# Neighbour maximum with one pick per source chunk and the other neighbours fetched from subset tables

## The chip, the cores and the metric

The kernel runs on one core of one Trainium2 chip. The metric is the device time of one launch in microseconds. A core has a matrix engine (PE, with a weight-load side, PEld), a vector engine (DVE), an activation engine (ACT), a general engine (POOL, which also issues indirect DMAs), a sync engine (SP, which issues the plain DMAs) and 16 DMA engines.

## The reference, cut to what matters

A graph of 4096 nodes with 128 features passes through two layers. `adj` is a symmetric 0/1 matrix, int32, with ones on its diagonal; a row has about 17 ones.

```python
h = relu(layernorm(x))
x = x + max over the neighbours j of node i of h[j]        # layer 0: out[i, d] = max_j adj[i, j] ? h[j, d] : -inf
h = relu(layernorm(x))
x = x + elu(softmax(leaky_relu(s_i + t_j), over adj[i] > 0) @ (h @ W))   # layer 1, s = h W a1, t = h W a2
```

## The kernel before, in words

**Stage one, the neighbour maximum.** The work is cut into 8 tiles of 512 target nodes, and each tile into 16 steps of 256 source nodes (two chunks of 128), so 128 steps, counted by `g` (PAIRS). A step goes through these hands:

- SP (L262 to L285) loads 512 targets x 512 sources of `adj` (1 MB) for every two steps, four loads ahead, and writes the turned edges (0.5 MB for two steps) to DRAM as `edge_units`, for stage two.
- PE `flip` (L574) transposes eight 128x128 blocks, and ACT `edges` (L386) turns them into 0/1 `edge_t`, sources on the partitions. PE `rank` (L589) multiplies with a triangular matrix, so that `order_ps` says how many edges stand above each edge in its chunk.
- ACT `select` (L393) makes from it `first` (the first edge of each target in each chunk, a one-hot selector) and `depth`. DVE `seconds` (L845) makes the selector `second`, and DVE `rests` (L852) and ACT `later` (L405), in turn, make `rest`: the edges that are neither first nor second.
- PE `pick(g, 0)` and `pick(g, 1)` (L598) multiply `first` and `second` with h in two fp16 halves (`h_hi`, `h_lo`), four 512-column matmuls each, and each pick is the feature row of one neighbour. DVE `take` (L858) raises the running maximum `acc` with each of the two (128x1024, float32); `fold` (L869) closes a tile.
- PE `digest` (L617) packs the rest edges of four chunks into one number for each position in a chunk: a word of four bits, 1024 words for each target. ACT `key` (L413) moves it to `keys` as the row number in a table. DVE `search` (L873) takes the 8 largest of the 1024 words of 128 targets with one MAX8.
- The table `subset_max` in DRAM holds the maximum of h over every subset of four rows. It is made in the first tile: DVE `chain` (L837), 11 maxima of 128x1024, and POOL, which writes it out (L335 to L347). POOL then fetches 6 rows for each target, as 6 indirect DMAs of 128 rows x 512 B for each block of 128 targets, paced by `raised`, the count of takes (L357 to L364). DVE `halve_two` and `halve` (L877, L891) reduce them to `left`, in a ring of NG = 4 blocks.

**Between the stages** the picks are transposed (`rows`, L631), merged with `left` (`merge`, L970), added to x and normalised again.

**Stage two, the attention**, is 256 steps `n` in the hand-written ORDER: DVE `weigh` (L1047) makes a 128x512 weight tile, and PE `mix` (L696) multiplies it with 129 columns of float32. DVE may be 6 tiles ahead (WEIGHTS). What is left of stage one is set between the steps by hand, in DVE's own order (L1083 to L1143): the searches of the last three blocks at n = 12, 33 and 44, joins at 19, 46, 56, 58, 62 and 68, `merge(6)` at 50. At the end a flag is summed up. If a row was not covered by its fetches, all engines enter a loop that does stage one again, one edge rank at a time.

Every engine works in program order. DVE's order is written by hand, so a wait in a `halve` holds back the `take` behind it; `pick` waits for the `take` that frees its PSUM buffer.

```python
pe.wait_ge(raised, 2 * (g - 1) + k + 1)                        # L609, in pick(g, k)
pool.wait_ge(raised, 2 * (STEPS + 2 + QUAD * n) + 4 + s)       # L359, the pace of the fetches
dve.wait_ge(gathered[b % NG][k], 16 * FETCHES // 2 * (b // NG + 1))   # L882, in halve_two
```

## Time and profile before

| | before |
|---|---|
| median of 3 runs | 742.18 us (742.01 to 743.37) |
| profiled execution, span | 753.0 us |
| PE busy | 681.6 us, 91% |
| DVE busy | 693.7 us, 92% |
| ACT busy | 473.1 us, 63% |
| POOL busy | 281.8 us, 37% |
| DMA moved | 163.07 MB |

The page gives one profiled execution: its span from the first to the last instruction is 753.0 us, and it states no other time of its own; the runs without a profile take 742.18 us. Busy time counts an engine's instructions, not its waits, and matmuls are shown longer than the spacing at which they follow each other, so spacings are read from the timeline. Stage one fills the first 27 of the 40 slices, stage two the others.

### The profile page before, as it was taken

The numbers are of one execution on the slowest core, as the hardware profiler recorded it, in microseconds if no ns is written. First come the engines' busy times: TensorE is split into PE (matmuls) and PEld (weight loads), VectorE is DVE, ScalarE is ACT, GpSimd is POOL, SyncE is SP. The second block draws the span as 40 slices with busy tenths as digits, with TensorE's granted clock in tenths as the row PEclk, the third lists the DMA queues.
The fourth block names the chain that finished last, engine by engine and source line by source line (L and its number), as shares of the span: only waits on it lengthen the run. The fifth ranks groups of instructions, "written<-read, shape, count | busy, mean of one in ns | idle before, by whom it ended". The sixth has DMA issues, their size and how long they took to land.

```text
span 753.0 us, 14749 instructions
## 1 busy us (share of the span) xinstructions
PE 681.6 (91%) x5560; PEld 490.6 (65%) x5560; DVE 693.7 (92%) x1023; ACT 473.1 (63%) x685; POOL 281.8 (37%) x259
## 2 busy tenths in 40 slices
PE   1788999999999999999999998699999999999994
PEld 1344655555555555555555554498998999999994
DVE  8999999999999999999999999988998999889893
ACT  3888999889898899998999897562433111001000
POOL 0612034434434535444444355441620294134040
PEclk9999999999999999999999999799999999999998
DMA  9999978997888888888888746342531544443400
GB/s 305 310 355 390 344 230 270 303 327 239 268 249 247 273 258 237 272 265 241 261 263 265 246 143 228 103 143 71 187 130 62 219 140 158 156 177 130 165 15 17
DMA packets 63000, 163.07 MB, mean 217 GB/s; under 512 B 6416, under 2 KB 11152, under 8 KB 58832
## 3 DMA queue, kind: packets, MB, share of 16 engines
q1 hardware_dynamic: 53776, 138.75, 54.2%
q0 software_dynamic: 9152, 23.34, 12.1%
q8 instruction: 47, 0.77, 0.4%
q14 instruction: 25, 0.20, 0.1%
HBM read 117.51 MB, written 44.56 MB: 215 GB/s over the span
## 4 chain that ended last, share of the span: by engine, by line
PE 53%; DVE 31%; issue 12%; ACT 2%; DMA 1%; DVEq 0%; another core or an unknown queue 0%; SPq 0%
PE pick_ps L714 23%; DVE acc L867 20%; PE pick_ps L613 17%; DVE rest L1054 5%; PE late_ps L627 4%; PE late_ps L585 4%; PE order_ps L594 2%; PE late_ps L693 1%; PE late_ps L623 1%; DMA best<-x 1%; DVE left L889 1%; ACT depth L403 1%; DVE found L915 1%; PE late_ps L714 1%; PE order_ps L680 1%
## 5 line engine op out<-in xcount | busy, mean ns | idle before, releaser
L867 DVE TENSOR_TENSOR acc<-pick_ps,acc 128x1024 f32<-128x1024 f32 x248 | 302.6, 1220 | 20.9 <-PE pick_ps L613 12.6
L363 POOL DMA_INDIRECT found<-subset_max,tops x192 | 204.4, 1065 | 271.8 <-DVE acc L867 187.5
L1054 DVE SCALAR_TENSOR_TENSOR rest<-depth,curves_sb,stage 128x512 f32<-128x512 f32 x256 | 199.5, 821 | 15.3 <-PE pick_ps L714 3.1
L714 PE MATMUL pick_ps<-keys,rest 128*128 128x129 f32 x1792 | 207.7, 276 | 3.3 <-DVE rest L1054 3.2
L714 PEld LDWEIGHTS pick_ps<-keys,rest 128*128 128x128 f32 x1792 | 204.6, 193 | 7.4 <-DVE rest L1054 5.8
L402 ACT ACTIVATE first<-order_ps 128x1024 f16<-128x1024 f32 x128 | 131.9, 1030 | 39.1 <-PE order_ps L594 33.0
L403 ACT ACTIVATE depth<-order_ps 128x1024 f16<-128x1024 f32 x128 | 131.5, 1027 | 0.0
L613 PE MATMUL pick_ps<-first,h_hi 128*128 128x512 f16 x256 | 97.3, 380 | 17.6 <-DVE acc L867 17.1
L613 PE MATMUL pick_ps<-second,h_hi 128*128 128x512 f16 x256 | 97.2, 380 | 15.2 <-DVE acc L867 14.7
L585 PEld LDWEIGHTS late_ps<-ident_h,stage 128*128 128x128 f16 x1024 | 68.4, 99 | 50.0 <-DMA stage<-adj 12.9
L613 PE MATMUL pick_ps<-first,h_lo 128*128 128x512 f16 x256 | 97.4, 380 | 0.0
L613 PE MATMUL pick_ps<-second,h_lo 128*128 128x512 f16 x256 | 97.3, 380 | 0.0
L585 PE MATMUL late_ps<-ident_h,stage 128*128 128x128 f16 x1024 | 80.2, 223 | 16.5 <-DMA stage<-adj 12.9
L594 PE MATMUL order_ps<-edge_t,order_w 128*128 128x512 f16 x256 | 77.6, 385 | 4.2 <-ACT depth L403 3.0
L391 ACT ACTIVATE edge_t<-late_ps 128x512 int32<-128x512 int32 x128 | 78.0, 610 | 4.2 <-PE late_ps L585 4.2
L627 PE MATMUL late_ps<-bit_w,rest 128*128 128x128 f16 x1024 | 78.4, 220 | 0.1
L516 ACT ACTIVATE keys<-pick_ps,acc 128x128 f32<-128x128 f32 x28 | 8.0, 367 | 97.7 <-DVE acc L1065 97.7
L613 PEld LDWEIGHTS pick_ps<-second,h_hi 128*128 128x128 f16 x256 | 24.8, 97 | 67.0 <-issue 45.5
L411 ACT ACTIVATE rest<-depth 128x1024 f16<-128x1024 f16 x64 | 68.3, 1067 | 0.0
L627 PEld LDWEIGHTS late_ps<-bit_w,rest 128*128 128x128 f16 x1024 | 64.4, 98 | 5.4 <-issue 0.8
L371 POOL TENSOR_SCALAR keys<-keys 128x512 f32<-128x512 f32 x7 | 12.9, 1845 | 111.2 <-ACT keys L516 111.1
L613 PEld LDWEIGHTS pick_ps<-first,h_hi 128*128 128x128 f16 x256 | 24.9, 97 | 39.4 <-issue 19.1
(146 smaller groups left out, 599.9 us busy)
## 6 DMA issues: line engine op xcount, KB each, us to landing
stage<-adj SPq DMA_DIRECT2D x64, 1024.0 KB
edge_units<-edge_t SPq DMA_DIRECT2D x64, 512.0 KB
stage<-edge_units SPq DMA_DIRECT2D x32, 1024.0 KB, 4.8
subset_max<-keys POOLq DMA_DIRECT2D x13, 512.0 KB, 9.0
found<-subset_max,tops POOLq DMA_INDIRECT x192
best<-x SPq DMA_DIRECT2D x4, 512.0 KB, 5.9
subset_max<-x POOLq DMA_DIRECT2D x4, 512.0 KB, 6.6
out<-keys POOLq DMA_DIRECT2D x7, 256.0 KB, 2.8
```

Source lines behind the costliest of these rows:

```text
L363: nc.gpsimd.indirect_dma_start(found[:, n % NG, s, :], None, subset_max, bass.IndirectOffsetOnAxis(tops[:, n, s:s + 1], 0)).then_inc(gathe ...
L391: nc.scalar.activation(edge_t[:, g % (KEPT * KEEP), :].bitcast(I32), flip_i[:, :], ACT.Copy, scale=ONE_BITS).then_inc(edge_ready, 1)
L402: nc.scalar.activation(first[:, g % 4, :], order_ps[:, :], ACT.Relu, scale=-1.0, bias=1.0 - MARK).then_inc(first_ready, 1)
L403: nc.scalar.activation(depth[:, g % 4, :], order_ps[:, :], ACT.Abs, bias=MARK - MID).then_inc(depth_ready, 1)
L411: nc.scalar.activation(rest[:, to, :], depth[:, g % 4, :], ACT.Sigmoid, scale=-SHARP, bias=SHARP * (MID - 1.5)).then_inc(rest_odd, 1)
L585: last = nc.tensor.transpose(flip_ps[:, c * TI + r * P:c * TI + (r + 1) * P], low[:, (s * PAIR + c) * P:(s * PAIR + c + 1) * P], ident_h[: ...
L594: last = nc.tensor.matmul(order_ps[:, c * TI:(c + 1) * TI], order_w[:, :], edge_t[:, g % (KEPT * KEEP), c * TI:(c + 1) * TI], start=True, ...
L613: last = nc.tensor.matmul(pick_ps[k][:, c * TI:(c + 1) * TI], half_h[:, p * PAIR + c, :], s[:, c * TI:(c + 1) * TI], start=part == 0, stop ...
L627: last = nc.tensor.matmul(key_ps[:, r * P:(r + 1) * P], rest[:, g % RESTS, c * TI + r * P:c * TI + (r + 1) * P], bit_w[:, b, :], start=n % ...
L714: last = nc.tensor.matmul(out_ps(q, b), weight[:, n % WEIGHTS, b * P:(b + 1) * P], wh[:, c, :], start=c == 0 and starts(q, b), stop=c == C ...
L867: V.tensor_tensor(acc[:, q % 2, :], pick_ps[k][:, :], acc[:, q % 2, :], ALU.max).then_inc(raised, 1)
L1054: V.scalar_tensor_tensor(out=weight[:, n % WEIGHTS, :], in0=limit[:, q % 4, :], scalar=slope[:, c:c + 1], in1=units[:, m % EDGES, k * TI:( ...
```

## The change

- `depth`, `second` and `rest` are gone. There is one pick per chunk (`pick(g)`), with two PSUM buffers in turn, and one `take` per step.
- The words are made of all edges minus the first ones: `digest` multiplies `edge_t` with `bit_w` and `first` with its negative `bit_n`, 16 small matmuls for each step in place of 8. The word numbers (`ones_h` with `word`, 512 columns) are added for every group of four chunks, not for every second one.
- `key` becomes a Relu with a sum beside it (`key_sums`), into a ring of eight 128x512 groups.
- The search goes by 512 sources: `maxes` takes the best 8 of 128 words for each block of 128 targets and each group (four MAX8 for two steps). `rank_words` then takes the best 8 of the 64 kept ones, makes row numbers of them, strikes them out (match_replace) and takes the next 8.
- 8 rows are fetched for each target in place of 6 (`SLOTS`), at most two fetches a step, and three for blocks 24 to 27, and the halving works on 8 slots.
- Rows with more than 8 words are listed apart ("spill"), in three parts (blocks 0 to 15, 16 to 23, 24 to 31): flags, counting matmuls, a permutation for each block (128x128, float32), a list of at most 128 rows for each part, 8 more fetches for the list, a scatter to DRAM, a load back and a maximum into `left`. The DRAM table `spill_max` is cleared by four more writes of 512 KB in the first tile.
- The flag for the loop at the end is raised if a row has 16 or more words, if a group held more than 8, or if a list is longer than 128.
- In stage two the order on DVE and PE moves: searches at n = 7, 11, 13, joins at 5, 33, 40, 46, 56, `merge(6)` at 58, spill steps at 14 to 18, 28, 50 and 58, and PE's `columns(6)` and `project(6)` from 60 and 63 to 66 and 69.

```diff
 SLOTS = 8
-FETCHES = 6
+RANKS = 16
...
+                for i in range(4):
+                    nc.gpsimd.dma_start(spill_dram[:, i * EIGHTH * 2:(i + 1) * EIGHTH * 2, :], spare(3)).then_inc(spill_clear, 16)
...
+                def spill_fetch(k):
+                    pool.wait_ge(spill_listed, k + 1)
+                    if k == 1:
+                        pool.wait_ge(spill_best, 1)
+                    for s in range(SLOTS):
+                        nc.gpsimd.indirect_dma_start(spill_found[k][:, s, :], None, subset_max,
+                                                     bass.IndirectOffsetOnAxis(spill_rows[:, k, s:s + 1], 0)).then_inc(spill_in, 16)
...
                 for n in range(C):
+                    q, r = n // ROWS, n % ROWS
+                    if n in (16, 24, 31):
+                        spill_fetch((16, 24, 31).index(n))
+                    if n in (18, 26):
+                        spill_store((18, 26).index(n))
+                    if n in (19, 27):
+                        spill_load((19, 27).index(n))
...
-                    pool.wait_ge(topped, n + 1)
+                    pool.wait_ge(ranked, n + 1)
                     if n >= NG:
                         pool.wait_ge(reduced, n - NG + 1)
-                    for s in range(FETCHES):
-                        if n < LAST * ROWS - 1:
-                            pool.wait_ge(raised, 2 * (STEPS + 2 + QUAD * n) + 4 + s)
+                    for s in range(SLOTS):
+                        if q < LAST:
+                            pool.wait_ge(raised, STEPS * (q + 1) + 4 + (r * SLOTS + s) // (2 if q < LAST - 1 else 3))
+                        elif n > LAST * ROWS or s >= 3:
+                            b, t = (n, s - 3) if s >= 3 else (n - 1, SLOTS + s - 3)
+                            pool.wait_ge(gathered[b % NG][t % 4], 32 * (b // NG) + 16 * (t // 4 + 1))
...
                 def select(g):
                     act.wait_ge(ordered, g + 1)
-                    nc.scalar.activation(first[:, g % 4, :], order_ps[:, :], ACT.Relu, scale=-1.0, bias=1.0 - MARK).then_inc(first_ready, 1)
-                    nc.scalar.activation(depth[:, g % 4, :], order_ps[:, :], ACT.Abs, bias=MARK - MID).then_inc(depth_ready, 1)
+                    if g >= FIRSTS:
+                        act.wait_ge(picked, g - FIRSTS + 1)
+                        act.wait_ge(digested, 2 * ((g - FIRSTS) // 2 + 1))
+                    nc.scalar.activation(first[:, g % FIRSTS, :], order_ps[:, :], ACT.Relu, scale=-1.0, bias=1.0 - MARK).then_inc(first_ready, 1)
...
                 def key(n):
                     act.wait_ge(digested, 2 * n + 2)
+                    if n >= KEYED:
+                        act.wait_ge(maxed, ROWS * (n - KEYED + 1))
+                    nc.scalar.activation(key_ring[:, n % KEYED, :], key_ps[:, :], ACT.Relu, bias=float(n % GROUPS - LEAST),
+                                         accum_out=key_sums[:, n:n + 1]).then_inc(keyed, 1)
...
+                def pick(g):
+                    pe.wait_ge(first_ready, g + 1)
+                    if g >= 2:
+                        pe.wait_ge(raised, g - 1)
...
                 def digest(n, half):
                     if half == 0:
-                        rest_done(pe, n)
+                        pe.wait_ge(first_ready, 2 * n + 2)
                         if n >= 1:
                             pe.wait_ge(keyed, n)
+                        nc.tensor.matmul(key_ps[:, :], ones_h[:, :], word[:, :].rearrange("p (r w) -> p r w", r=1).broadcast_to((P, ROWS, P)), start=True, stop=False)
                     for r in range(half * ROWS // 2, (half + 1) * ROWS // 2):
                         for b in range(QUAD):
+                            nc.tensor.matmul(key_ps[:, r * P:(r + 1) * P], edge_t[:, g % (KEPT * KEEP), at:at + P], bit_w[:, b, :], start=False, stop=False)
+                            last = nc.tensor.matmul(key_ps[:, r * P:(r + 1) * P], first[:, g % FIRSTS, at:at + P], bit_n[:, b, :],
+                                                    start=False, stop=r == ROWS - 1 and b == QUAD - 1)
...
+                    if g in (74, 106):
+                        pe.wait_ge(keyed, g // 2)
+                        spill_count((74, 106).index(g))
+                        pe.wait_ge(spill_seen, (74, 106).index(g) + 1)
+                    if g in (80, 110):
+                        pe.wait_ge(keyed, g // 2)
+                        spill_list((80, 110).index(g))
+                        pe.wait_ge(spill_listed, (80, 110).index(g) + 1)
...
+                def maxes(n, half):
+                    q, g = n // GROUPS, n % GROUPS
+                    dve.wait_ge(keyed, n + 1)
+                    for r in range(half * ROWS // 2, (half + 1) * ROWS // 2):
+                        V.max(best_words[:, q % 2, r, g * SLOTS:(g + 1) * SLOTS], key_ring[:, n % KEYED, r * P:(r + 1) * P]).then_inc(maxed, 1)
...
+                def rank_words(n):
+                    sort_step(V.max(tops[:, n, 0:SLOTS], of))
+                    sort_step(V.scalar_tensor_tensor(out=vacant[:, 1, :], in0=tops[:, n, 0:SLOTS], scalar=0.0, in1=vacant[:, 0, :], op0=ALU.is_equal, op1=ALU.mult))
+                    V.scalar_tensor_tensor(out=rows_at[:, n, :], in0=tops[:, n, 0:SLOTS], scalar=float(LEAST), in1=vacant[:, 1, :],
+                                           op0=ALU.add, op1=ALU.add).then_inc(ranked, 1)
+                    sort_step(V.match_replace(of, tops[:, n, 0:SLOTS], of, -1.0))
+                    sort_step(V.max(tops[:, n, SLOTS:RANKS], of))
...
                 for g in range(PAIRS):
+                    take(g)
+                    if g >= 3:
+                        maxes((g - 3) // 2, (g - 3) % 2)
+                    if q >= 1 and 3 <= p < 7:
+                        rank_words(ROWS * (q - 1) + p - 3)
+                    if q >= 1 and p >= 13 and q < LAST:
+                        halve(ROWS * (q - 1), 2, p - 13)
+                    if q >= 2 and 5 <= p < 8:
+                        halve(ROWS * (q - 2) + 2, 2, p - 5)
+                    if q == LAST and 11 <= p < 14:
+                        halve(ROWS * (q - 1), 2, p - 11)
+                    if g in (88, 121):
+                        spill_join((88, 121).index(g))
```

## Rows read from the trace of the kernel before

**Rows 1.** The page: span, busy time of each engine, and the chain that ended last.
```profile
span 753.0 us, 14749 instructions
PE 681.6 (91%) x5560; PEld 490.6 (65%) x5560; DVE 693.7 (92%) x1023; ACT 473.1 (63%) x685; POOL 281.8 (37%) x259
PE 53%; DVE 31%; issue 12%; ACT 2%; DMA 1%; DVEq 0%; another core or an unknown queue 0%; SPq 0%
```

**Rows 2.** Windows: us, PE, PEld, DVE, ACT, POOL busy (instructions), granted clock, DMA share, GB/s.
```profile
60.00:70.00 10.00, 8.61 (x73) 4.92 (x72) 9.90 (x11) 8.29 (x12) 1.60 (x3) 1.00 1.04 405
...
140.00:160.00 20.00, 18.38 (x144) 10.21 (x142) 18.82 (x20) 17.51 (x24) 8.15 (x9) 1.00 1.02 336
...
341.60:355.40 13.80, 12.80 (x107) 7.26 (x105) 12.40 (x13) 12.44 (x17) 6.25 (x6) 1.00 0.83 257
```

**Rows 3.** DVE around step 80: timeline from 306 us (start, length), and all folds.
```profile
306.48 1.22 DVE L867 TENSOR_TENSOR acc<-pick_ps,acc 128x1024 f32<-128x1024 f32 x1
307.61 0.68 DVE L850 TENSOR_SCALAR second<-depth 128x2048 f16<-128x2048 f16 x1
...
312.21 0.69 DVE L871 TENSOR_TENSOR best<-acc 128x512 f32<-128x512 f32 x1
...
L871 DVE TENSOR_TENSOR best<-acc x8: 682/686/687, 90.6 to 539.6; 128x512 f32<-128x512 f32 x8
```

**Rows 4.** PE in one step: timeline from 312.84 us, and eight weight loads.
```profile
312.84 0.38 PE L613 MATMUL pick_ps<-second,h_hi 128*128 128x512 f16 x1
...
313.70 0.61 PE L585 MATMUL late_ps<-ident_h,stage 128*128 128x128 f16 x8
314.15 0.61 PE L627 MATMUL late_ps<-bit_w,rest 128*128 128x128 f16 x8
314.60 0.38 PE L613 MATMUL pick_ps<-first,h_hi 128*128 128x512 f16 x1
...
461.90 0.65 PEld L627 LDWEIGHTS late_ps<-bit_w,rest 128*128 128x128 f16 x8
```

**Rows 5.** Groups of instructions by line: busy us, mean ns, idle before. DVE and ACT.
```profile
L402 ACT ACTIVATE first<-order_ps 128x1024 f16<-128x1024 f32 x128 | 131.9, 1030 | 39.1 <-PE order_ps L594 33.0 <-issue 3.2 <-remote 1.9
L391 ACT ACTIVATE edge_t<-late_ps 128x512 int32<-128x512 int32 x128 | 78.0, 610 | 4.2 <-PE late_ps L585 4.2
L875 DVE MAX8 tops<-keys 128x8 int32<-128x1024 f32 x32 | 39.0, 1218 | 0.0
L985 DVE BATCH_NORM_STATS2 acc<-x 128x6 f32<-128x128 f32 x32 | 6.9, 281 | 0.0
L1002 DVE TENSOR_TENSOR acc<-acc 128x4 f32<-128x4 f32 (+1 forms) x6 | 1.0, 164 | 0.2
```

**Rows 6.** DMA queues on the page, and the fetches on POOL (group by line, then timeline).
```profile
q1 hardware_dynamic: 53776, 138.75, 54.2%
...
L363 POOL DMA_INDIRECT found<-subset_max,tops x192 | 204.4, 1065 | 271.8 <-DVE acc L867 187.5 <-issue 44.3 <-DVE tops L875 20.7
...
316.63 0.95 POOL L363 DMA_INDIRECT found<-subset_max,tops  x1 [0.92 <-DVE acc L867]
317.89 0.95 POOL L363 DMA_INDIRECT found<-subset_max,tops  x1 [0.31 <-issue]
...
531.19 4.34 POOL L363 DMA_INDIRECT found<-subset_max,tops  x1 [0.96 <-DMA found<-subset_max,tops]
```

**Rows 7.** The chain that ended last, in order of time: the first and the last take.
```profile
27.36 1.23 DVE acc L864
...
477.10 1.23 DVE acc L867
```

**Rows 8.** Stage two: DVE's timeline at its start and before n = 72, and a stretch of PE's chain.
```profile
486.11 1.42 DVE L1054 SCALAR_TENSOR_TENSOR rest<-depth,curves_sb,stage 128x512 f32<-128x512 f32 x2
...
569.72 8.04 DVE L1054 SCALAR_TENSOR_TENSOR rest<-depth,curves_sb,stage 128x512 f32<-128x512 f32 x12
...
663.72 28.58 PE pick_ps L714 x256
```

More of the change, by code:

```diff
@@ L747, in _ @@
                 rows(3)
-                for half in range(2):
-                    digest(PAIRS // 2 - 1, half)
                 project(0)
@@ new lines, in spill_cuts @@
+                def spill_cuts(k, lo, hi):
+                    first_block, end = SPILLS[k]
+                    dve.wait_ge(spill_seen, k + 1)
+                    if k == 1 and lo == first_block:
+                        dve.wait_ge(spill_done, 1)
+                    for n in range(lo, hi):
+                        last = V.tensor_scalar(spill_perm[k][:, n - first_block, :], places[:, :], spill_at[:, n:n + 1], None, ALU.is_equal)
+                    if hi == end:
+                        last.then_inc(spill_cut, 1)
@@ new lines, in _, with halve @@
+                halves = [0]
+                def halve(n, blocks, i):
+                    at = slice(n % NG, n % NG + blocks)
+                    if i == 0:
+                        for b in range(n, n + blocks):
+                            for k in range(4):
+                                dve.wait_ge(gathered[b % NG][k], 32 * (b // NG + 1))
+                        V.tensor_tensor(found[:, at, 0:4, :], found[:, at, 0:4, :], found[:, at, 4:8, :], ALU.max).then_inc(halved, 1)
+                        halves[0] += 1
@@ L1041, in _ @@
                 scales(1)
+                maxes(QUADS - 2, 1)
+                for half in range(2):
+                    maxes(QUADS - 1, half)
                 def cap(q):
```

386 lines of the change are left out of this document (210 added, 176 removed).

## The prediction

> **What bounds the kernel now.** I read the page first: PE and DVE are each busy for over nine tenths, and the chain that ended last runs mostly over these two [rows 1]. A share over 753 us says nothing of a stage, so next the folds: DVE closes a tile at 90.6 us and another, four tiles later, at 312.21 [rows 3], so 16 steps take 55.4 us and a step 3.46. Stage one runs from the first take at 27.4 to the last at 477.1 us [rows 7], 60% of the span, and nearly all of the change is there.
>
> Then what each engine needs for a step. PE, from its timeline [rows 4]: four 512-column matmuls take 0.86 us (0.215 each) and sixteen 128-column ones 0.90 (0.056 each). Ten large and sixteen small make 3.05, and a quarter of a word matmul 0.05: 3.10 us. DVE: a take follows the last after 1.13 us (307.61 less 306.48) [rows 3]; two takes, half a `second`, a quarter each of a `rest` and a MAX8 and the halving make 3.3, and with a gap where two takes follow each other, 3.46: **DVE bounds the step**, PE is 10% behind, ACT has two activations of 1.03 us, one of 0.61, half a `key` (taken as 0.61, since it is as wide) and half a `later` of about 1.03: 3.5 by durations and less by spacing [rows 5]. DMA is busy at 0.83 in the steady windows [rows 2].
>
> **What the change makes of a step.**
> - PE: four pick and two rank matmuls, 6 x 0.215 = 1.29; 8 flips and 16 digests, 24 x 0.056 = 1.34; half a word matmul, 0.11. Together **2.74 us**. The second pick goes (0.86) and 8 small matmuls come (0.45).
> - DVE: one take 1.14. `maxes` adds two MAX8 of 128 columns. Not in the trace; from below it is bounded by the smallest operation (0.16), from above by MAX8 of 1024 (1.22) [rows 5]. Nearest is the 128-column statistics, 0.28 long; I take 0.21 as spacing, 0.42 a step. `rank_words` has five small operations that wait for each other, 64 columns or 8; match_replace is not in the trace, between 0.16 and 1.22, nearest the small end. I take 1.1 to 1.3 us for a block, 0.3 a step. Halving on 8 slots, two pairs of blocks a tile: 2 x 2.1 us = 0.26 a step, and the fold 0.04. Together **2.2 us**. The trace shows no DVE bound left, though it bunches at p = 5 and 6 to 3.8 us.
> - ACT: 1.03 + 0.61 + 0.31 and a sum beside the key, unseen, between nothing and a second pass of 0.62 for two steps: **2.0 to 2.3**.
> - DMA: the plain queue moved 138.75 MB in 54.2% of 753 us, so 340 GB/s while busy [rows 6]. A step's `adj` and edges are 0.786 MB, 2.31 us at full share. The window at 0.83 of 3.46 us holds 2.87, which leaves 0.56 for 1.5 fetches, 0.37 each. Two fetches make 2.31 + 0.75 = 3.06. The share has gone to 1.04 (405 GB/s) and 1.02 with fetches (336 GB/s) [rows 2], so **2.9 us**, with 2.26 as the low end (0.917 MB at 405 GB/s).
> - POOL: a fetch takes 1.065 us and waits 0.30, and back to back it is 1.26 (317.89 less 316.63) [rows 6]. Two a step: **2.5 to 2.7 us**.
>
> So PE 2.74, DMA 2.9 and POOL 2.6 take DVE's place, all within a tenth. I take 2.9 for a step; the ends are 2.74 and 3.1.
>
> **The sum, stage one.**
> 1. Start: ACT leaves out three `depth` before the first pick, but the scaling of x on DVE holds it nearly as long: -1.5 us (bounds -2.8 and +1 for the new constants).
> 2. First tile, 63.2 us to the fold. The tables (17 x 0.524 MB) and the new clearing (2.1 MB) go through the same queues as 17 steps of 0.786 MB; four loads (4.2 MB) may be used up. 20.2 MB at 385 GB/s (a little under the 405 of [rows 2]) are 52.5 us: -10.5. Bounds: 46.6 by PE, 63 unchanged.
> 3. 96 steps to the fold before the last tile: 6 x 55.4 = 332.4 against 278.4: -54.
> 4. Fetches behind the list. `spill_fetch` puts 8 fetches ahead of block 16, and POOL has no slack. From take 82 it needs 8 x 1.0 + 16 x 1.27 + about 3 us to land = 31.3; DVE reaches the halving of block 16 at step 93 after 29.6: +2 to +3. In the last tile the same 31.3 us stand against 8.15 steps (22.8 us), since halving is at p = 11: DVE waits **8.5 us** before the take behind it, and so does PE.
> 5. List on PE: counting 16 and 8 tiny matmuls (1.3), listing 24 float32 ones at 0.22 (5.3; by the float32 pace of stage two, 28.58 us for 256 halves [rows 8]), waits for DVE behind them 2.5: 9 us. DMA goes on loading meanwhile; I keep half, +4.
> 6. The last 15 steps: 54.1 us before (477.1 less the fold at 90.6 + 332.4); 42 + 9 (from 4) + 2 for the merges: -1.
>
> Stage one: -1.5 - 10.5 - 54 + 3 + 4 - 1 = **-60 us**.
>
> **Stage two.** DVE goes from 486.1 to 569.7 without rest [rows 8]: it bounds the first 72 steps, PE the others (256 halves in 28.58 us, 0.89 a step against 0.67 to 0.75 on DVE). Removed from DVE there: three MAX8 (3.7), six joins of 1.2, the old flag: 12 us. Added: three `rank_words` 3.6, five joins 9.5, eight 128x128 cuts 2, take and join of the list 2.4, `spill_merge(2)` 1.2, the flag's eight operations 1.8, marks 0.4: 21. Of the 9 to 10 more I count 8; later PE has no slack to give them back. Before n = 0 come six `maxes` and `spill_merge(1)`: +2.5. If POOL's last fetches come late, `spill_merge(2)` holds DVE another 0 to 6; I take 0. Together **+10.5 us** (4 to 18).
>
> **Sum:** -49.5. The profiled execution has a span of 753.0 us, 10.8 over the median of 742.18; I carry the difference over unscaled: 742.2 - 49.5 = 692.7, said as **693**. A measurement can tell about 0.2%, 1.5 us, from no change.
>
> **Rivals.**
> - **A, PE alone is the bound.** The DMA share is packet time, not a limit; packets overlap, and 405 GB/s has been seen. Then a step is 2.76, the 96 steps save 67.5, the first tile 14, and POOL keeps up: 742 - 1.5 - 14 - 67.5 + 9 + 4 - 3 + 6 = **675**; with stage two nearly unchanged, 668. Chance 0.27.
> - **B, DMA fetches get dearer when it is full.** A share of 1.04 then costs each fetch 0.5, a step is 3.15, each halving waits: 111 steps x 0.25 over the forecast: **720**. For it: one fetch took 4.34 us [rows 6]. Chance 0.1.
> - **C, slower.** POOL's fetches set the pace of DVE: every `halve` stands ahead of a `take`, and POOL is in order. From a spacing of 1.7 us for a fetch on (a step of 3.35, 49 us over 111 steps) the gain is gone; at 1.9 the time is 742 + 43 = **785**. Against it: 1.26 to 1.37 in the trace. Chance 0.04.
> - **D, weight loads bound the small matmuls.** Eight loads stand in the trace over 0.65 us [rows 4], 0.08 each, more than the 0.056 of the matmuls. In a run of 24 they could be what counts: 24 x 0.08 + 1.40 = 3.3 us a step, 111 x 0.4 over the forecast, **737**. Against it: sixteen in a row kept 0.056 [rows 4]. Chance 0.03. The Trainium skill (TensorE: Matmul & The Clock Gate, Back-to-back issue gap) says that a stream of weight loads and matmuls is held at about 81 ns for each of 128 columns; by that rule PE would come to 3.34 us. The trace disagrees for runs of sixteen, and no row shows 24.
> - **E, the loop at the end runs.** It would be milliseconds. Counted from the inputs as the reference draws them (seed 0): no row has over 15 words left (16 would trip it), no group over 8, the three lists hold 69, 33 and 32 of 128. Chance 0.01.
>
> **How the numbers follow.** The forecast's own case, 680 to 710, has 0.55; A 0.27, B 0.10, C 0.04, D 0.03, E 0.01. The range goes from A's lower end to B: **668 to 720**. It leaves out C, D, E and tails of A and B. Slower by over 0.2%: C, E and a little of D, 0.06. Within 0.2%: D's edge, 0.01. Faster: 0.93.
>
> **What would show it.** The folds of the steady tiles stand 46 us apart (44 says A, 50 says B). DVE is busy for about 0.75 in those windows, PE 0.9 and over, the DMA share over 0.95. MAX8 of 128 columns is about 0.25 long. Matmuls of 128 columns keep 0.056 in a run of 24. POOL fetches stand at 1.26 to 1.4, and DVE waits for fetches near step 123 for some 8 us. Between the first weigh and n = 72 lie some 8 us more than before. I am wrong if PE waits in the steady tiles for something other than `adj`, or if folds stand over 52 us apart.

## The result and the profile after

The changed kernel takes **738.35 us** (730.74 to 744.51, 11 runs) against 742.48 us (741.95 to 743.37, 11 runs) of the kernel before: a ratio of 0.9905, 95% interval 0.9882 to 0.9929, so faster by 0.7 to 1.2%. Two of the eleven runs, 741.78 and 744.51 us, lie over 1.5% above the fastest and are left out of the ratio; the other nine have a median of **735.48 us**, and it is this that the experiments below are set against. The sign was right; 693 us was not, nor was the range. Of 49.5 us foreseen, 4 came by the first median and 7 by the second.

The page of the changed kernel: span, busy time, queues, the chain that ended last, and groups.

```profile
span 736.6 us, 15876 instructions
...
PE 643.8 (87%) x6200; PEld 525.3 (71%) x6200; DVE 564.0 (77%) x1296; ACT 306.1 (42%) x554; POOL 366.4 (50%) x357
...
q1 hardware_dynamic: 53776, 138.75, 53.9%
q0 software_dynamic: 13072, 33.51, 16.7%
...
PE 52%; DVE 15%; DMA 14%; POOL 11%; issue 7%; ACT 1%; DVEq 0%; SPq 0%; POOLq 0%; ACTq 0%
...
L409 POOL DMA_INDIRECT found<-subset_max,rows_at x256 | 256.6, 1002 | 143.0 <-issue 58.9
...
L918 DVE MAX8 best_words<-keys 128x8 f32<-128x128 f32 x256 | 61.0, 280 | 0.1
...
found<-subset_max,rows_at POOLq DMA_INDIRECT x256, 6.7
```

Beside [rows 1], DVE has lost 130 us of work (693.7 to 564.0), as meant, and PE 38. But the chain, of which DMA was 1%, is now DMA for 14% and POOL for 11%. The last line has what the forecast put at 3 us without a row: a fetch of words lands 6.7 us after its issue (median).

The folds, which close a tile of 16 steps, now start at 85.44, 134.58, 183.70, 227.59, 272.79, 329.37 and 382.33 us. Two of them in DVE's timeline, with the waits that stand between two others:

```profile
183.70 0.68 DVE L912 TENSOR_TENSOR best<-acc 128x512 f32<-128x512 f32 x1
...
227.59 0.68 DVE L912 TENSOR_TENSOR best<-acc 128x512 f32<-128x512 f32 x1
...
308.79 0.69 DVE L970 TENSOR_TENSOR limit<-limit 128x512 f32<-128x512 f32 x1 [6.99 <-DMA limit<-subset_max,spill_rows]
...
323.12 1.23 DVE L988 TENSOR_TENSOR found<-found 128x1024 f32<-128x1024 f32 x1 [3.41 <-DMA found<-subset_max,rows_at]
...
329.37 0.69 DVE L912 TENSOR_TENSOR best<-acc 128x512 f32<-128x512 f32 x1
```

The tile from 183.70 takes 43.9 us, 2.74 a step, where one of before took 55.4 [rows 3] (53.65 in e0 below). The tile from 272.79 to 329.37 takes 56.6. Windows over both, over the start, and over a stretch of the last tile (us, PE, PEld, DVE, ACT, POOL busy with instructions, granted clock, DMA share, GB/s):

```profile
50.00:60.00 10.00, 3.23 (x13) 1.58 (x14) 6.12 (x9) 0.47 (x1) 1.07 (x2) 0.52 1.03 415
...
183.70:227.60 43.90, 43.90 (x492) 31.62 (x490) 34.42 (x82) 29.69 (x49) 31.11 (x32) 1.00 1.00 338
272.80:329.40 56.60, 50.88 (x537) 36.84 (x537) 35.97 (x88) 30.12 (x50) 40.15 (x39) 0.97 0.93 282
...
420.00:430.00 10.00, 5.28 (x30) 4.36 (x31) 3.24 (x5) 1.13 (x4) 7.96 (x10) 0.53 0.79 301
```

In the good tile PE is busy all the time, DVE for 0.78, and the DMA share is 1.00 at 338 GB/s. In the first and the last window PE stands still for a good part, and its granted clock is near the lower level, 1.2 GHz (0.52 and 0.53 of 2.4). The waits of the whole span (engine, line, waited for: us in total, times, longest):

```profile
PE pick_ps L638 <- DVE acc L908: 18.4, 6, 11.1
PE pick_ps L756 <- DVE weight L1174: 18.3, 14, 3.9
DVE found L988 <- DMA found<-subset_max,rows_at: 26.0, 6, 12.4
DVE keys L897 <- DMA subset_max<-keys: 14.3, 1, 14.3
DVE limit L970 <- DMA limit<-subset_max,spill_rows: 9.3, 2, 7.0
PE late_ps L779 <- POOL acc L399: 8.0, 1, 8.0
```

DVE waits some 50 us for transfers, and PE for DVE behind it.

### The profile page after: what moved, and what is told of

Read it like the earlier page. It is cut to its first block, busy times and chain, and to the rows that moved or that the text cites. A ratio compares the mean times of both kernels' runs of the same rounds, so it can differ in the third digit from the quotient of the medians.

```text
span 736.6 us, 15876 instructions
## 1 busy us (share of the span) xinstructions
PE 643.8 (87%) x6200; PEld 525.3 (71%) x6200; DVE 564.0 (77%) x1296; ACT 306.1 (42%) x554; POOL 366.4 (50%) x357
## 4 chain that ended last, share of the span: by engine, by line
PE 52%; DVE 15%; DMA 14%; POOL 11%; issue 7%; ACT 1%; DVEq 0%; SPq 0%; POOLq 0%; ACTq 0%
PE pick_ps L756 20%; PE pick_ps L638 10%; POOL found L409 7%; DMA found<-subset_max,rows_at 5%; PE late_ps L651 5%; PE late_ps L652 5%; PE late_ps L614 5%; PE order_ps L623 5%; DVE weight L1174 4%; DMA edge_units<-edge_t 4%; DVE acc L908 3%; DMA subset_max<-keys 2%; PE late_ps L647 1%; DMA limit<-subset_max,spill_rows 1%; POOL h_lo L349 1%
## 5 line engine op out<-in xcount | busy, mean ns | idle before, releaser
L409 POOL DMA_INDIRECT found<-subset_max,rows_at x256 | 256.6, 1002 | 143.0 <-issue 58.9
L756 PE MATMUL pick_ps<-keys,weight 128*128 128x129 f32 x1792 | 214.5, 281 | 18.3 <-DVE weight L1174 18.3
L756 PEld LDWEIGHTS pick_ps<-keys,weight 128*128 128x128 f32 x1792 | 209.6, 197 | 23.8 <-DVE weight L1174 21.9
L1174 DVE SCALAR_TENSOR_TENSOR weight<-limit,curves_sb,stage 128x512 f32<-128x512 f32 x256 | 199.8, 821 | 14.5 <-PE pick_ps L756 2.0
L908 DVE TENSOR_TENSOR acc<-pick_ps,acc 128x1024 f32<-128x1024 f32 x120 | 146.5, 1221 | 69.3 <-PE pick_ps L638 68.5
L652 PE MATMUL late_ps<-bit_n,first 128*128 128x128 f16 x1024 | 131.5, 222 | 0.0
L651 PE MATMUL late_ps<-bit_w,edge_t 128*128 128x128 f16 x1024 | 131.4, 222 | 0.0
L614 PEld LDWEIGHTS late_ps<-ident_h,stage 128*128 128x128 f16 x1024 | 69.5, 100 | 60.8 <-ACT edge_t L440 14.6
L652 PEld LDWEIGHTS late_ps<-bit_n,first 128*128 128x128 f16 x1024 | 101.8, 99 | 8.2 <-issue 0.6
L651 PEld LDWEIGHTS late_ps<-bit_w,edge_t 128*128 128x128 f16 x1024 | 101.7, 99 | 0.4
L440 ACT ACTIVATE edge_t<-late_ps 128x512 int32<-128x512 int32 x128 | 76.1, 595 | 38.5 <-PE late_ps L652 23.8
L918 DVE MAX8 best_words<-keys 128x8 f32<-128x128 f32 x256 | 61.0, 280 | 0.1
```

What stands on the lines that cost most here:

```text
L409: nc.gpsimd.indirect_dma_start(found[:, n % NG, s, :], None, subset_max, bass.IndirectOffsetOnAxis(rows_at[:, n, s:s + 1], 0)).then_inc(ga ...
L440: nc.scalar.activation(edge_t[:, g % (KEPT * KEEP), :].bitcast(I32), flip_i[:, :], ACT.Copy, scale=ONE_BITS).then_inc(edge_ready, 1)
L614: last = nc.tensor.transpose(flip_ps[:, c * TI + r * P:c * TI + (r + 1) * P], low[:, (s * PAIR + c) * P:(s * PAIR + c + 1) * P], ident_h[: ...
L651: nc.tensor.matmul(key_ps[:, r * P:(r + 1) * P], edge_t[:, g % (KEPT * KEEP), at:at + P], bit_w[:, b, :], start=False, stop=False)
L652: last = nc.tensor.matmul(key_ps[:, r * P:(r + 1) * P], first[:, g % FIRSTS, at:at + P], bit_n[:, b, :], start=False, stop=r == ROWS - 1 a ...
L756: last = nc.tensor.matmul(out_ps(q, b), weight[:, n % WEIGHTS, b * P:(b + 1) * P], wh[:, c, :], start=c == 0 and starts(q, b), stop=c == C ...
```

## The experiments

Two causes stood against each other: the list of fuller rows as a whole (made on PE and DVE, fetched by POOL) takes the gain back, or the step itself is dearer than its parts. The times are medians of runs, each beside runs of the kernel before (medians 742.47 to 743.14 us) on the same chip; ratios are against it. "Tiles" are the distances of the seven folds; "end" is the last take less the last fold; "two" is the span from the first weigh on. These three come from one profiled execution of each kernel. Runs of one changed kernel lie up to 9 us apart, so differences of 2 or 3 us between two kernels, or in one tile between two traces, tell little.

| kernel | us | ratio (95%) | tiles | end | two |
|---|---|---|---|---|---|
| e0_before | 742.58 | | 52.6 53.7 54.0 53.7 53.6 53.6 | 55.8 | 266.3 |
| after | 738.35 (735.48) | 0.9905 (0.9882 to 0.9929) | 49.1 49.1 43.9 45.2 56.6 53.0 | 56.5 | 287.7 |
| e1_no_list | 682.59 | 0.9184 (0.9161 to 0.9207) | 43.9 50.9 43.9 43.9 43.9 43.9 | 44.3 | 273.1 |
| e8_list_only | 703.66 | 0.9487 (0.9462 to 0.9512) | 47.4 50.8 43.9 45.0 49.4 49.1 | 44.3 | 278.2 |
| e9_fetch_only | 711.64 | 0.9576 (0.9556 to 0.9596) | 50.1 49.6 43.9 43.9 51.2 45.1 | 57.4 | 276.1 |
| e11_six | 714.21 | 0.9604 (0.9589 to 0.9619) | 46.2 49.5 43.9 45.0 55.1 48.0 | 45.1 | 283.9 |
| e4_clear_late | 731.67 | 0.9865 (0.9834 to 0.9895) | 45.8 47.8 43.9 45.1 55.6 49.1 | 56.9 | 287.4 |
| e13_wide_and_halves | 732.47 | 0.9855 (0.9822 to 0.9889) | 47.1 49.3 43.9 45.0 57.8 52.9 | 42.4 | 289.7 |
| e10_all_four | 721.94 | 0.9715 (0.9696 to 0.9734) | 43.9 43.9 43.9 45.0 56.9 48.5 | 56.7 | 287.6 |
| e14_all_six | 716.83 | 0.9639 (0.9614 to 0.9665) | 44.5 43.9 43.9 45.0 57.1 51.1 | 42.3 | 286.2 |

**e0_before**, the kernel before once more, to have a second trace of it.

> The kernel before, unchanged, profiled once more. Its one profile has a span of 753.0 us, while its runs without a profile take 742.5; the changed kernel's span (736.6) and time (738.5) agree. If that first profile was of a longer execution, this one has a span of 740 to 742 us, and its folds and the start of stage two tell which stage was longer in the first. If profiling itself costs this kernel 11 us, the span is again 753.

Its span is 740.5 us, not 753.0. The tile that took 55.1 us in the profile ahead of the prediction takes 53.65 here:

```profile
251.76 0.68 DVE L871 TENSOR_TENSOR best<-acc 128x512 f32<-128x512 f32 x1
...
305.41 0.68 DVE L871 TENSOR_TENSOR best<-acc 128x512 f32<-128x512 f32 x1
```

The profile that the sum was worked against was of a longer execution: a step is 3.35 us, not 3.46.

**e1_no_list.** All calls around the list go, from the clearing of its room to the merges.

```diff
-                if n in (16, 24, 31):
-                    spill_fetch((16, 24, 31).index(n))
...
-                    if g in (74, 106):
-                        spill_count((74, 106).index(g))
...
-                    if g == 102:
-                        spill_merge(0)
```

> The changed kernel without the list of fuller rows (left out: clearing, counting, permutations, 24 list fetches, scatter, load back and the maximum into left; rows with more than 8 words keep their first 8). Theory Q, the queues: what the forecast missed is that fetches land late and stand in one queue behind the list's, so DVE waits before a take (7.0, 3.4, 2.9 and 12.4 us in stage one, 5.6, 3.5, 1.8 in stage two) and PE with it. Then the time falls by 25 to 40 us, to about 700 to 712, and the tiles after step 80 take 44 us like the tile of steps 48 to 64. Theory D, the load on the DMA engines: only the list's bytes matter (some 5 MB, 13 us, mostly hidden), the waits for fetches stay, and the time falls by less than 15 us, to 724 or more.

682.59 us: the list costs **52.9 us** (735.48 - 682.59), over seven times what the change as a whole gains, and more than either theory said. Between the two traces, whose spans are 736.6 and 680.4 us, it is 40.6 us until the last take (438.87 against 398.27), 41.6 to the first weigh (448.88 against 407.25), and 14.6 behind it (287.7 against 273.1). Without the list four tiles in a row stand at the same distance:

```profile
266.16 0.68 DVE L883 TENSOR_TENSOR best<-acc 128x512 f32<-128x512 f32 x1
...
310.04 0.68 DVE L883 TENSOR_TENSOR best<-acc 128x512 f32<-128x512 f32 x1
```

**e8_list_only and e9_fetch_only** split it. The first makes the list on PE and DVE and neither fetches nor merges. The second makes no list and stores none: at the list's places it fetches the rows of blocks 0, 16 and 24 once more, joins them, loads the cleared table back and merges it.

```diff
-                    if n in (16, 24, 31):
-                        spill_fetch((16, 24, 31).index(n))
...
-                    dve.wait_ge(spill_done, spill_of(g) + 1)
```
```diff
-                    pool.wait_ge(spill_listed, k + 1)
+                    if k < 2:
+                        pool.wait_ge(raised, (81, 111)[k])
...
-                    if g in (74, 106):
-                        spill_count((74, 106).index(g))
```

> The changed kernel with the list made on PE and DVE as before (flags, counting, permutations, row numbers) and nothing done with it: the 24 list fetches, the scatter, the load back, the joins and the merges are left out, the clearing stays. Without the whole list the time is 682.6, with it 738. If PE's and DVE's waits for each other around the list are what costs (theory P), most of the 56 us stay: 710 to 725. If it is the fetches in POOL's queue and DVE's waits for them (theory Q), 695 to 708: 7 for the clearing and 6 to 16 for PE and DVE.

> The other half: the list's 24 fetches, joins, load back and merges stay at their places (with rows of blocks 0, 16 and 24 fetched a second time, as numbers), the clearing too, and the counting, permutations and row numbers on PE and DVE and the scatter are left out. Theory Q: 720 to 732, most of the 56 us. Theory P: 692 to 705.

703.66 us is what theory Q said for e8; 711.64 for e9 lies between the two theories. Added to e1, the list's making costs 21.1 us and these fetches 29.1, each with the clearing, which both keep. Taken from the changed kernel, the fetching is worth 31.8 us (735.48 - 703.66) and the making 23.8. Both are causes. With the clearing counted once (3.8 us, by e4 below) 21.1 and 29.1 make 46.4, and the list costs 52.9. In the tile from step 80 the one adds 5.5 us, the other 7.3, both 12.7. In the last tile the fetching alone does it: 44.3 us without, 57.4 with.

e9 doesn't fetch what the list fetches, and the traces tell the two apart. In the changed kernel the last of the first list's eight fetches is issued at 296.31 and DVE goes on at 308.79, 12.5 us later; in e9 it is issued at 290.40 and DVE goes on at 296.58, 6.2 later. Meanwhile the DMA engines are as busy in both and move half the bytes in the first: between 282 and 312 us no window of 10 us has under 332 GB/s in e9. The changed kernel, e9, and windows of the two:

```profile
296.31 0.95 POOL L372 DMA_INDIRECT limit<-subset_max,spill_rows  x1 [0.30 <-issue]
...
290.40 0.94 POOL L375 DMA_INDIRECT limit<-subset_max,rows_at  x1 [0.30 <-issue]
...
296.58 0.69 DVE L957 TENSOR_TENSOR limit<-limit 128x512 f32<-128x512 f32 x1 [0.67 <-DMA limit<-subset_max,rows_at]
...
292.00:302.00 10.00, 10.00 (x109) 6.96 (x106) 9.38 (x27) 6.68 (x12) 7.87 (x8) 1.00 0.99 184
...
292.00:302.00 10.00, 10.00 (x109) 6.94 (x107) 8.88 (x18) 6.49 (x12) 7.71 (x8) 1.00 1.01 346
```

e8, which makes the list and doesn't fetch it, has 0.98 at 330 GB/s there, so it isn't the making. What differs in the kernel is the rows that are asked for. `rows_at` gives every empty place a row of its own (`vacant`); `spill_rows` gives all empty places the same one, and with 69 of 128 places filled (rival E's count) that is at least 472 of the first list's 1024 row numbers. That this makes its fetches slow is argued, not shown: no run spreads them.

**e3_unpaced** takes away the wait of the last blocks' fetches for earlier ones.

```diff
-                        elif n > LAST * ROWS or s >= 3:
-                            b, t = (n, s - 3) if s >= 3 else (n - 1, SLOTS + s - 3)
-                            pool.wait_ge(gathered[b % NG][t % 4], 32 * (b // NG) + 16 * (t // 4 + 1))
```

> The changed kernel without the pace of the last four blocks' fetches (each waited for the landing of the third before it); nothing left out. A fetch lands in 5 to 6 us here, so three in flight give one every 1.9 us, against 1.26 back to back. Theory Q: blocks 28 to 31 are through some 15 us earlier, the waits of 5.6 and 1.8 us near n = 56 go, and the time falls by 3 to 8 us, to 730 to 735. If stage two is longer because of DVE's added work alone, the time stays within 2 us.

733.41 us (0.9889, 0.9863 to 0.9915): 2 us under the changed kernel, whose interval (0.9882 to 0.9929) it overlaps. The pacing is worth little or nothing of the 52.9.

**e4_clear_late** moves the four writes that clear the list's room out of the start into the loop over blocks.

```diff
+                    if n in (4, 6, 8, 10):
+                        i = (n - 4) // 2
+                        nc.gpsimd.dma_start(spill_dram[:, i * EIGHTH * 2:(i + 1) * EIGHTH * 2, :], spare(3)).then_inc(spill_clear, 16)
```

> The changed kernel with the four clearing writes of 2 MB in all put from the first tile to POOL's turns before blocks 4, 6, 8 and 10; nothing left out. With the list gone altogether the first two tiles took 83.6 and 43.9 us against 85.4 and 49.1 with it, and that part of the list is only the clearing. If the burst in the first tile is what costs, this gives back 5 to 7 us (about 732). If the bytes cost wherever they are (DMA engines full), less than 2.

731.67 us, 3.8 less, and its interval (0.9834 to 0.9895) still touches that of the changed kernel. The tile from step 16 falls from 49.1 to 45.8, but kernels that leave the clearing where it was have 46.2 to 50.1 there. So by this run the burst costs something between nothing and 7 us; e10 below, where that tile takes 43.9, speaks for some of it. The first fold comes only 0.6 us earlier, so its 85 us have another cause.

**e5_chains** spreads the joins of the tables over more steps, and **e6_x_late** loads x again in 16 small parts from step 56 on, not in one at step 32.

```diff
-                    if g < len(CHAINS):
-                        chain(g)
+                    if g in CHAIN_AT:
+                        chain(CHAIN_AT.index(g))
```
```diff
-                    if n == UNITS * 4:
...
-                        sp.dma_start(hs[:, :, :], x_rows).then_inc(x1_in, 16)
+                    if n >= 28 and n % 2 == 0 and n < 60:
...
+                        sp.dma_start(hs[:, 2 * i:2 * i + 2, :], x_rows[:, 2 * i:2 * i + 2, :]).then_inc(x1_in, 16)
```

> The changed kernel with the 11 chains of the subset tables at steps 0, 1, 2, 3, 5, 7, 8, 10, 11, 13 and 14 in place of 0 to 10; nothing left out. In the first tile DVE waits 14.3 us in one piece for a table's write before a chain, with the takes behind it, and PE's clock falls to 1.2 GHz. If the chains' density is what makes that wait, the first tile is 6 to 12 us shorter and the time 729 to 733. If the tile is bound by the bytes through the DMA engines (20 MB, 52 us), its fold stays near 85 us and the time within 3 us of 738.

> The changed kernel with the second load of x (2 MB in rows of 512 B, at once at step 32) put to 16 loads of 128 KB at steps 56 to 118; nothing left out. A tile with that load takes 49 to 51 us, its neighbours 43.9. If the burst holds back the edge writes, and ACT and PE behind them, 4 to 6 us come back (about 733). If the same bytes cost the same anywhere, since POOL's fetches and the DMA engines are full at every step, the time stays within 2 us.

e5 gives 735.91 us (0.9901, 0.9882 to 0.9921), which can't be told from the changed kernel, though its first fold is at 82.34: a miss. e6 gives 732.25 (0.9837, 0.9817 to 0.9858), 3.2 us less by the medians and 5 by the ratios, and its tile from step 32 takes 43.9, not 49.1. That tile was long in e1 too (50.9), so it has nothing to do with the list: with the one large load ACT waits there for an edge write (4.1 us in the changed kernel, 5.0 in e1) and PE behind it, and in e6 neither does.

**e7_no_low** leaves out the low half of the picks, so that PE needs 2.31 us a step.

```diff
-                        for part, half_h in enumerate((h_hi, h_lo)):
...
+                        last = nc.tensor.matmul(pick_ps[g % 2][:, c * TI:(c + 1) * TI], h_hi[:, p * PAIR + c, :],
```

> The changed kernel with the low half of h left out of the picks (two of four 512-column matmuls in each step), so that PE needs 2.31 us a step in place of 2.74. The tile of steps 48 to 64 took 43.9 us, which is 16 x 2.74. If PE alone bounds a step there, it now takes 37 us. If the DMA engines, whose share is 1.00 there, bound it as well (the forecast's 2.9 or just under the 2.74 seen), it stays at 42 to 44 us.

729.82 us in its one run. The good tile doesn't move; its window:

```profile
179.70:223.50 43.80, 38.95 (x460) 28.16 (x458) 33.96 (x82) 29.09 (x49) 32.58 (x32) 1.00 1.00 345
```

PE is busy for 0.89 and the tile is as long as before. Something else stands right behind PE: POOL issues its 32 fetches back to back,

```profile
205.31 0.96 POOL L409 DMA_INDIRECT found<-subset_max,rows_at  x1 [0.30 <-issue]
206.57 0.96 POOL L409 DMA_INDIRECT found<-subset_max,rows_at  x1 [0.31 <-issue]
207.83 0.96 POOL L409 DMA_INDIRECT found<-subset_max,rows_at  x1 [0.30 <-DVE acc L907]
```

1.26 us apart (206.57 less 205.31), so 40.3 of 43.8 us, and the DMA share is 1.00. Which of the two holds it, this run doesn't say. With both halves of h the limit is PE: e11 below has only 24 fetches in that tile, and it takes 43.9 us with PE busy all the time there too.

**e11_six**, without the pacing, fetches 6 of the 8 words, and leaves out the seventh and eighth.

```diff
-                    for s in range(SLOTS):
+                    for s in range(SLOTS - 2):
```

> The changed kernel without pace in the last blocks (733.4) and with 6 rows fetched for each target in place of 8 (the seventh and eighth are left out); the list stays whole. POOL then needs 1.9 us of each step's 2.74 in place of 2.5. If the list's fetches cost because POOL has no room left for them (theory Q), DVE's waits for fetches shrink to under 8 us and the time is 708 to 718. If the list costs by its own length on PE and DVE (theory P), it stays over 724.

714.21 us, 19.2 under e3 (733.41): with 24 fetches a tile, POOL has room for the list. (It also fetches 4.2 MB less, and this run doesn't part the two.) The end takes 45.1 us in place of 56.5, and DVE's wait for words is gone. The tile from step 80 stays at 55.1 us, so there it isn't POOL's room that counts: 5.5 us are the making of the list, by e8, and 4.0 DVE's wait for its fetches, which makes 9.5 of the 11.2 over a good tile.

**e2_late_halves** puts the halving that DVE waits 12.4 us for behind the last take, and the first list's join, for which it waits 7.0 us, four steps later.

```diff
-                    if q == LAST and 11 <= p < 14:
-                        halve(ROWS * (q - 1), 2, p - 11)
...
-                    if g in (88, 121):
+                    if g in (92, 121):
...
+                join(C - 8, 2)
```

> The changed kernel with two DVE steps put later, nothing left out: the halving of blocks 24 and 25 goes from steps 123 to 125 to just before the first weigh, and the first list's join from step 88 to 92. Theory Q: the waits of 12.4 us and of 7.0 us go, or turn up later at half their length, because the fetches themselves are not faster: time 4 to 16 us less, 722 to 734. If DVE's waits are harmless because PE would have waited for adj anyway (theory D), the time stays within 3 us of 738.

738.86 us (0.9941, 0.9922 to 0.9960): **nothing** gained, a clear miss, although both long waits are gone. The timelines of its ACT and PE say why:

```profile
307.51 0.60 ACT L440 ACTIVATE edge_t<-late_ps 128x512 int32<-128x512 int32 x1 [5.26 <-DMA edge_units<-edge_t]
...
423.10 1.19 PE L779 MATMUL late_ps<-acc 128*128 128x256 f32 x2 [7.21 <-POOL acc L399]
```

At the list's join ACT now waits 5.3 us for an edge write to DRAM, DVE gets its next pick 8.0 us late, and the tile takes 58.0 us where it took 56.6. In the changed kernel ACT waits 2.8 us for that write, under DVE's 7.0. In the last tile PE stands in the same stretch for two small POOL operations (L398, L399) that widen the attention vector. They need no fetch, but POOL is in order, and the list's 8 fetches, 16 fetches of words and the store are ahead of them. Here is how the changed kernel has it, first POOL, then PE and DVE:

```profile
420.52 0.94 POOL L409 DMA_INDIRECT found<-subset_max,rows_at  x1 [0.30 <-issue]
421.77 1.00 POOL L379 DMA_INDIRECT spill_max<-limit,spill_rows  x1 [0.31 <-issue]
422.82 0.63 POOL L398 TENSOR_SCALAR acc<-ones,a 128x128 f32<-128x128 f32 x1
...
424.17 1.19 PE L779 MATMUL late_ps<-acc 128*128 128x256 f32 x2 [8.00 <-POOL acc L399]
...
426.76 1.28 DVE L988 TENSOR_TENSOR found<-found 128x1024 f32<-128x1024 f32 x1 [12.36 <-DMA found<-subset_max,rows_at]
```

The last of the words is issued at 420.52 and lands 6.12 us later by the chain. Two waits lie over each other, and four more runs asked whether that is all.

**e12_wide_early** moves the two operations ahead of the words; **e13_wide_and_halves** does that and e2's edit.

```diff
-                    if n == LAST * ROWS - 2:
+                    if n == LAST * ROWS - 4:
```

> The changed kernel, with POOL's two small operations that widen the attention vector (L398, L399) moved two blocks ahead on POOL's queue: behind the list's second 8 fetches but before the 16 word fetches and the store that now stand ahead of them. In the trace of the changed kernel PE waits 8.0 us for them at 424.17, over the same stretch in which DVE waits 12.4 us for fetches to land (426.76). Theory H (two waits lie over each other there, so taking either away gives nothing): PE's wait goes, DVE's stays, the time is 736 to 740 us. Theory J (PE's wait is the one that sets the end): 728 to 732 us.

> The same move of the two operations, together with the late halving of e2_late_halves, which alone gave nothing; there DVE's wait of 12.4 us was gone and PE waited 7.2 us for the two operations. Theory H: with both waits away the last tile is about 7 us shorter, and the time is 729 to 733 us. Rival (the halving that is put off costs as much before stage two as its wait did, since the last take to the first weigh grew from 10.0 to 12.7 us there): 736 to 740 us.

e12 gives 737.16 us (0.9912, 0.9894 to 0.9930), nothing: PE's wait for POOL is gone and DVE's is longer.

```profile
426.51 1.23 DVE L988 TENSOR_TENSOR found<-found 128x1024 f32<-128x1024 f32 x1 [14.31 <-DMA found<-subset_max,rows_at]
```

e13 gives 732.47 us, 3.0 less than the changed kernel and 6.4 less than e2. Each edit alone gives nothing. Both together stand apart from e2 (0.9889 against 0.9922), just touch the changed kernel (0.9889 and 0.9882), and stand apart in e14 against e10, below. The end falls by 14.1 us, from 56.5 to 42.4, but from the last take to the first weigh it is 18.2 us where it was 10.0: 8 of the 14 are paid back, by the halving that was put off and by what now stands there.

**e10_all_four** is e3, e4, e5 and e6 together, with nothing left out; **e15_five** adds e12's edit, **e14_all_six** e2's as well.

> Four changes of order together, nothing left out: clearing late (-6.7 us alone), fetches of the last blocks without pace (-5.0 alone), chains apart, x late. If their gains add: 713 to 722, at least 20 us under the kernel before. If the freed queues only move the waits, 724 to 730.

> The kernel of e10_all_four with the early widening alone. By the trace of that kernel PE waits 7.24 us at 407.18 and DVE 11.9 us at 410.04, overlapping. Theory H: 720 to 722.5 us, no change. Theory J: 714 to 716 us.

> The kernel of e10_all_four with both of these edits. Theory H: 4 to 7 us under its 721.9, so 715 to 718 us. Rival: 720 to 724 us.

e10 gives 721.94 us, e15 722.92 (0.9741, 0.9728 to 0.9754), no better than e10, as for e12 (e2's edit was not tried alone on top of e10). e14 gives **716.83 us** (711.21 to 717.72), 3.6% under the kernel before and 18.7 us under the changed one, and is the version to take. Its first three tiles are at 44.5, 43.9 and 43.9. Its span is 34.2 us over that of e1: the tile from step 80 (57.1) and the next (51.1) make 20.5, stage two 13.1, and the stretch from the last take to the first weigh 9.1, less what its first tiles and its end save. In DVE's timeline behind the last take stands this:

```profile
424.38 1.22 DVE L979 TENSOR_TENSOR left<-left,weight 128x1024 f32<-128x1024 f32 x1 [5.71 <-DMA weight<-spill_max]
```

DVE stands for the list's rows to come back from memory.

**Stage two** of the changed kernel shows waits behind its third list too, in DVE's timeline (for the count on PE, for words, for the rows to come back):

```profile
476.25 0.17 DVE L947 SCALAR_TENSOR_TENSOR spill_at<-order_ps,spill_flag 128x8 f32<-128x8 f32 x1 [3.49 <-PE order_ps L661]
...
524.04 0.69 DVE L988 TENSOR_TENSOR found<-found 128x512 f32<-128x512 f32 x1 [5.57 <-DMA found<-subset_max,rows_at]
...
528.69 1.23 DVE L978 TENSOR_TENSOR left<-left,first 128x1024 f32<-128x1024 f32 x1 [1.85 <-DMA first<-spill_max]
```

Together 10.9 us. They need not all be on the path, but between these traces the list costs 14.6 us there. The stage takes 284 to 292 us in the kernels with the whole list and 273 without.

## Why the prediction was wrong, by its steps

**What held.** The bound of before, DVE, went. PE's terms were exact: 2.74 us a step were counted, and 43.9 / 16 is 2.74. DVE is busy for 34.42 / 16 = 2.15 us a step, 2.2 was said. MAX8 of 128 columns takes 0.28 us, and two of them 0.48 in the timeline, 0.20 apart where 0.21 was taken. Of `rank_words`, the search and replacement takes 0.084 and 0.208 us, near the small end. ACT's sum costs 0.204 for two steps. POOL's fetches stand 1.26 us apart.

**Item 3, the DMA share.** It was priced at 2.9 us a step, above PE. The good tile runs at a share of 1.00 with 338 GB/s and PE never waits, so rival A was right on the step: 2.74. With that alone stage one would have been 15 us shorter than forecast. e7 shows that POOL or DMA stands close behind.

**Rival D** falls. In PE's timeline 24 matmuls of 128 columns in a row, from the first flip to the next pick, take 89.14 - 87.80 = 1.34 us:

```profile
87.80 0.61 PE L614 MATMUL late_ps<-ident_h,stage 128*128 128x128 f16 x8
88.24 0.22 PE L651 MATMUL late_ps<-bit_w,edge_t 128*128 128x128 f16 x1
...
89.08 0.22 PE L652 MATMUL late_ps<-bit_n,first 128*128 128x128 f16 x1
89.14 0.38 PE L638 MATMUL pick_ps<-first,h_hi 128*128 128x512 f16 x1
```

That is 0.056 each. The rule of the Trainium skill weighed there (TensorE: Matmul & The Clock Gate, Back-to-back issue gap), about 81 ns, is not borne out by this kernel's runs of 24 either.

**Items 4 and 5, the list: the step that failed.** They were priced at 3, 8.5 and 4 us, some 15 in stage one. The clearing adds 5 by its bytes, and the list's part of stage two some 7 (2 + 2.4 + 1.2 + 0.4 and a merge of 1.2): 28 us in all. Measured, the list is 41.6 us up to the first weigh and 14.6 behind it. Four things were wrong or missing.

- The two tiles from step 80 were to lose 3 + 4 us between them, and lose 21.8 (109.5 us against 87.8 in e1). The wait was looked for where DVE halves block 16, at step 93, and the join of the list itself at step 88 was put at nothing. DVE waits 7.0 us there.
- The list's eight fetches were priced at 1.0 us each and 3 to land. They take 11.1 us (286.50 to 297.57), and the last lands 12.5 us after its issue. For the 3 us there was no row; words land in 6.7 us here, and e0's page has 6.5, so the change didn't make that longer.
- POOL's queue also holds two operations that PE needs in the last tile, and the change put 8 fetches of the list, 4 more of words and a store ahead of them.
- Half of PE's 9 us for the list was taken to be hidden, while in e8 the two lists cost 5.5 and 5.2 us in their tiles. Nor was it counted that PE is slower behind a stop: after the first list's matmuls, from 276.76 to 278.47 us, 16 matmuls of 128 columns take 0.107 us each and not 0.056, at a granted clock of 0.50.

The mean granted clock is 0.956 here, 0.975 in e1, 0.992 in e0. What that is worth over the whole span I can't part from the stops themselves.

The DMA page of the Trainium skill (DMA: Bandwidth & Descriptors, Anatomy of one DMA, SWDGE path) gives a POOL-issued transfer about 2 us and the time of its bytes. By that a 64 KB fetch would land after an estimated 2.2 us. The trace agrees where the queues are nearly empty: the 25 fetches between 440 and 480 us, at 95 GB/s, land in 2.6 us (median). In stage one it doesn't, with 6.6 us in the good tile.

**Item 2, the first tile.** From the first take to the fold -10.5 us was said; against e0 it is -4.2 (59.6 against 63.8). DVE waits 14.3 us for a table to be written (L897), PE stops behind it, and the clock falls to 0.52 at a DMA share of 1.03. e1, without the clearing, needs 58.0, so most of the gap is the tables' own.

**Two tiles too long** (49.1 and 49.1) were in no step. The second is the one load of x (e6). The first takes 43.9 only without the burst of the clearing (e1, e10), which e4 alone didn't settle.

**Stage two.** +10.5 was said, with a bound of 18, and it took in what stands before the first weigh. From the last take on it is +25.7 (297.7 us against 272.0 in e0). Without the list it is +10.1.

**The base.** The sum took 3.46 us for a step of before; e0 has 3.35. Over 111 steps that is 12 us of gain that was never there. I carried 10.8 us of difference between the profile and the runs over unscaled, while nearly all of it lay in the steps that the change removes. And 477.1 us is the last take on the chain, not the last take, which starts at 479.72.

Put together, by the traces of e0 and of the changed kernel (spans 740.5 and 736.6):

| stretch | said | measured | missed by |
|---|---|---|---|
| start, to the first take | -1.5 | -1.9 | -0.4 |
| first tile | -10.5 | -4.2 | 6.3 |
| next six tiles | -54 + 3 + 4 | -24.3 | 22.7 |
| last steps of stage one | -1 | +0.8 | 1.8 |
| from the last take on | +10.5 | +25.7 | 15.2 |

That is 45.6, and 692.7 + 45.6 = 738.3. The 22.7 of the six tiles are 11 for the base, less 15 for the step, 7 for the load of x, and 19.5 for the list and its clearing (26.5 against e1, 7 said). The list as a whole is 56 us between the traces where 28 were foreseen. Without it the forecast would have been 665, and the time is 682.6: with the list priced right it would still have missed by 18.

Rival C, POOL's fetches pace DVE, came nearest in its mechanism, a DVE that waits for fetches on an in-order queue, and had 0.04. It was priced by the spacing of fetches (1.26, as it stayed) and not by the room left on the queue: 40.3 of a tile's 43.9 us are taken, and a list brings ten entries more.

## What to carry to other kernels

When a change fills an in-order queue to nine tenths, price its rare work (a list, an exception) as what is pushed back behind it, every consumer of that queue included, and take the landing time of a transfer from a stretch as loaded as the one that it will stand in. Look at which rows a rare gather asks for in its empty places, too. Where two engines wait over the same stretch, taking one wait away can give nothing and says nothing against the cause: read the other engine's timeline there and take both. Before a step's length is multiplied by a hundred, read it in a second profile of the kernel before.

## What the runs showed of the hardware

- A fetch of 64 KB by rows, issued by POOL, lands in 6.7 us (median) in this kernel and in 2.6 between 440 and 480 us, where little else moves. The list's clearing writes, 0.5 MB each, land in 14.0 us behind the tables and in 7.4 in e10.
- A DMA share of 1.00 is no sign of a bound by itself: 338 GB/s fed a PE that never waited for it, and 415 GB/s went through at 1.03. It is no measure of the bytes either: at 0.99 only 184 GB/s went through while the list was fetched.
- Spreading 2 MB of loads over a longer stretch gave 3 to 5 us, with the same bytes (e6); for 2 MB of writes 3 to 4 us stand within the noise (e4).
- Left open: whether the one row that all empty places ask for is what makes the list's fetches slow, what the falls of the clock cost by themselves, and what in the tables' writing holds the first tile.
